# Trainium2: inverse roots of the second and third norm by a power instruction on POOL instead of nine steps on DVE, in a one-core MetaFormer block

## The chip, the cores and the metric

The program runs on one core of one Trainium2 chip. A core has a matrix engine (PE, with its weight loads shown apart as PEld), a vector engine (DVE), a scalar engine (ACT), a general engine (POOL, also called GpSimd) and a queue engine that issues transfers (SP). The engines run side by side and wait for one another by semaphores. The metric is the time of one execution on the device, in microseconds (us).

## The reference, cut to what matters

The input x is 8 images of 64 channels and 32x32 pixels. All in float32:

```python
x = x + conv_attention(ln_over_channels(x, eps=1e-6))      # first norm
t = to_tokens(x)                                            # [8, 1024, 64]
u = layer_norm(t, eps=1e-5)                                 # second norm
rw = softmax(mean(u, axis=1) @ Wr + br)                     # routing of each image over 8 experts
rw = softmax(rw * min(1, capacity / load))
top_w, top_i = top_k(rw, 2); top_w = softmax(top_w)
y = sum_k top_w[k] * (gelu(u @ W1[e_k] + b1[e_k]) @ W2[e_k] + b2[e_k])
out = t + layer_norm(y + u, eps=1e-5) * gamma + beta        # third norm
```

A layer norm subtracts the mean over the 64 channels and multiplies with 1 / sqrt(variance + eps). Attention is over channels: the scores of a head are 8x8.

## The kernel before, in words

The eight images are handled as four pairs p (NP = 4, two images side by side on the 128 partitions, 1024 pixels along the free axis). A norm is over channels, so over partitions. Its sums come out of PE (moment_rows, L888, then transposes, moment_columns, L895) as moments with tokens on the partitions, 16 numbers for each partition and pair (G2 = 16). DVE makes a variance of them, and then an inverse root.

- rsqrt (L511) is nine dependent instructions on DVE, L515 to L525: a shift and a subtraction on the bits for a first guess, a cubic step, and a Newton step. Each waits for the one before through a semaphore (link, L503), which can run other work in that gap (the argument between).
- split3 (L207) cuts the root into three bf16 parts, four instructions L210 to L213. PE transposes them (turn, L912, matmul L913), DVE copies them to RR (rows2, L618, rows3, L779), and PE spreads them over the channels (spread, L924, matmul L927).
- The second norm is done in two groups g of two pairs, 32 columns each. read_moments (L600) writes scaled moments, rstd2 (L609) squares the mean (L611), takes the variance (L612) and calls rsqrt, with residual1 of pair 3 (T, L597) in two gaps for group 0 and rows2(0) in one gap for group 1. POOL's split_group (L422) waits for each root. normal2 (L624, L626) multiplies T with the spread root: UF, with its sum in su. ACT rounds UF to f16 (HI, L308), POOL subtracts (LO, L419), SP copies HI and LO to ST. sw (L697) takes the sums of all pairs and starts the routing (L701 to L747), at whose end POOL gathers the weights of the chosen experts (L437 to L452). PE has 18 filler matmuls (keep_awake, L958, matmul L966) between the sum over tokens (L1027) and the first expert.
- The expert stage is written out by hand in steps (L1109 to L1135): up (L1041, L1053), GELU on ACT (L362), down (L1071, L1080), and among them the third norm of the pair before. ACT squares (L376), PE sums (L891), ACT evacuates (L383), PE transposes (L897), and DVE's rstd3 (L767) makes v (L770) and the root. For pairs 0 to 2 POOL splits it, for pair 3 DVE does (L805). Then rows3, bias2 (L749, L753: the bias of pair p + 2), and scale_z (L785, L788), in the order of DVE's loop from L792. evac_z (L764) takes the expert sums out of PSUM.
- add_residual (L215, L220) adds T to the result, 512 columns at a time, and SP stores each half (L255), waiting in order of pairs and halves. POOL adds all halves of pairs 0 to 2 and half 0 of pair 3; DVE adds the last half.
- Before the last turn PE has nine filler matmuls (keep_awake_at_end, L1086, matmul L1088), before the one of pair 2 seven.

Every engine executes its own list in order. On POOL the list around the change is: split_group(0), split_group(1), LO of pairs 0 and 1, gathers, LO of pairs 2 and 3, and then the loop from L480: gather, split of pair p, additions of pair p - 1.

Of the kernel before, what the change touches and what calls it, by code (L numbers as in the profile page):

```python
# [51 lines left out]
def build_program(nc, x_tok, x_cha, small, w12, consts, constb, out):  # L52
# [11 lines left out]
    with ExitStack() as ctx:  # L64
        def sb(name, shape, dt=F32):
            return ctx.enter_context(nc.sbuf_tensor(name, shape, dt))
# [33 lines left out]
        p1s = sb("p1s", [P, 2, 2, C])  # L100
# [8 lines left out]
        cbs = sb("cbs", [P, NP])  # L109
# [2 lines left out]
        cmp2 = sb("cmp2", [P, 2, 4, 2 * G2])  # L112
        seed = sb("seed", [P, 2 * G2], U32)
        nwt = sb("nwt", [P, 2, 2 * G2])
        r2 = sb("r2", [P, NP, G2])
        v3 = sb("v3", [P, NP, G2])
        r3 = sb("r3", [P, NP, G2])
# [36 lines left out]
        def by_half(ap):  # L154

            return ap.rearrange("p (q h b) -> p h q b", h=2, b=2)
# [16 lines left out]
        def pair_view(ap):  # L173
# [22 lines left out]
        s_sq = [sem(f"s_squared{p}") for p in range(NP)]  # L196
        s_st = [sem(f"s_st{p}") for p in range(NP)]
        s_out = [sem(f"s_out{p}") for p in range(NP)]
        names = ("ones clear onesm wrb sw wcp wcv gram gs tb u p1 p1s s_ps sms exs a_sb b1 b1s mt mts cbs conv t "
                 "row rw mom pow1 pow2 red2 r3 rt rr rb uf hi lo w1p w1h w1l w2p w2v lg rexp1 rexp2 "  # L200
                 "half_tanh rx1 rx2 rx3 wkd top "
                 "g1 g2 c2d mm1 gelu mm2 zs sq3 row3 rw3 mom3 red3 pow3 s3 rt3 rr3 rb3 vv tbeta dve pool").split()
# [4 lines left out]
        def split3(engine, link, b, n, src, done):  # L207

            to = slice(b, b + n)
            link(engine.tensor_copy(R3[:, to, 0, :], src))  # L210
            engine.tensor_tensor(rd[:, to, :], src, R3[:, to, 0, :], ALU.subtract)
            link(engine.tensor_tensor(R3[:, to, 1, :], src, R3[:, to, 0, :], ALU.subtract))
            engine.tensor_tensor(R3[:, to, 2, :], rd[:, to, :], R3[:, to, 1, :], ALU.subtract).then_inc(done, 1)  # L213

        def add_residual(engine, queue, p, h):  # L215

            queue.wait_ge(s["vv"], 2 * p + h + 1)
            queue.wait_ge(s["tbeta"], p + 1)
            cols = slice(h * HALF, (h + 1) * HALF)
            engine.tensor_tensor(OUT[:, p, cols], V[:, p, cols], T[:, p, cols], ALU.add).then_inc(s_fin[2 * p + h], 1)  # L220
# [180 lines left out]
        def _(pool):  # L401
# [18 lines left out]
                                        ALU.subtract).then_inc(s["lo"], 1)  # L420

            def split_group(g):  # L422
                pool.wait_ge(s["pow2"], g + 1)
                if g >= 1:
                    pool.wait_ge(s["rt"], g)
                split3(nc.gpsimd, link, 0, 2, r2[:, 2 * g:2 * g + 2, :], s["r3"])
# [16 lines left out]
            def gather_w2(p, regs):  # L443
# [4 lines left out]
                for k in range(TOP):  # L448
                    for b in range(2):
# [2 lines left out]
                        nc.gpsimd.tensor_tensor(w2g[:, p % 2, b, k, :], w2c[:, bass.ds(e * C, C)],  # L452
                                                wrep.broadcast_to([P, C]), ALU.mult).then_inc(s["g2"], 1)

            nc.gpsimd.memset(ones_m[:, :], 1.0).then_inc(s["onesm"], 1)
            nc.gpsimd.memset(wrbd[:, :], 0.0).then_inc(s["onesm"], 1)
            pool.wait_ge(s["onesm"], 2)
# [22 lines left out]
            for p in range(NP):  # L480
                if p + 2 < NP:
                    gather_w2(p + 2, gather_b1(p + 2))
                if p == NP - 1:
                    break
                pool.wait_ge(s["pow3"], p + 1)
                if p >= 2:
                    pool.wait_ge(s["rt3"], p - 1)
                else:
                    pool.wait_ge(s["rt"], 2)
                split3(nc.gpsimd, link, p % 2, 1, r3[:, p:p + 1, :], s["s3"])  # L490
                if p >= 1:
                    add_residual(nc.gpsimd, pool, p - 1, 0)
                    add_residual(nc.gpsimd, pool, p - 1, 1)
            add_residual(nc.gpsimd, pool, NP - 2, 0)
            add_residual(nc.gpsimd, pool, NP - 2, 1)
            add_residual(nc.gpsimd, pool, NP - 1, 0)


        @block.vector
        def _(dve):  # L500
            count = [0]

            def link(ins, between=None):  # L503

                count[0] += 1
                ins.then_inc(s["dve"], 1)
                if between:
                    between()
                dve.wait_ge(s["dve"], count[0])
# [90 lines left out]
            def read_moments(p):  # L600

                dve.wait_ge(s["mom"], p + 1)
                g, cols = p // 2, slice(p % 2 * G2, (p % 2 + 1) * G2)
                pm = moments_of(moment_bank[p % 2])
                nc.vector.tensor_scalar(by_half(cmp2[:, g, 0, cols]), pm[:, 0], RSQRT ** 0.5 / S_U, None, ALU.mult)
                nc.vector.tensor_scalar(by_half(cmp2[:, g, 1, cols]), pm[:, 1], RSQRT / S_U ** 2,
                                        RSQRT * EPS_T / S_U ** 2, ALU.mult, ALU.add).then_inc(s["red2"], 1)

            def rstd2(g, between=None):  # L609
                dve.wait_ge(s["red2"], 2 * (g + 1))  # L610
                link(nc.vector.tensor_tensor(cmp2[:, g, 2, :], cmp2[:, g, 0, :], cmp2[:, g, 0, :], ALU.mult))  # L611
                link(nc.vector.tensor_tensor(cmp2[:, g, 3, :], cmp2[:, g, 1, :], cmp2[:, g, 2, :], ALU.subtract))  # L612
                if g >= 1:
                    dve.wait_ge(s["pow2"], g)
                rsqrt(cmp2[:, g, 3, :], nwt[:, 0, :], nwt[:, 1, :], seed[:, :],
                      r2[:, 2 * g:2 * g + 2, :].rearrange("p l g -> p (l g)"), s["pow2"], between)

            def rows2(g):  # L618
                dve.wait_ge(s["rt"], g + 1)
                if g >= 1:  # L620
                    dve.wait_ge(s["rb"], 2 * g)
                nc.vector.tensor_copy(RR[:, :, :].rearrange("p l n -> p (l n)"), ps_rt2).then_inc(s["rr"], 1)
# [41 lines left out]
            def residual_between():  # L664

                calls[0] += 1
                if calls[0] in (1, 3):
                    residual1(3, [calls[0] // 2])

            rstd2(0, residual_between)  # L670
            read_moments(2)
            read_moments(3)
            calls[0] = 0

            def rows_between():
                calls[0] += 1
                if calls[0] == 1:
                    rows2(0)

            rstd2(1, rows_between)  # L680
            normal2(0)
            rows2(1)
            normal2(1)
# [83 lines left out]
            def rstd3(p):  # L767
                dve.wait_ge(s["mom3"], p + 1)
                pm = moments_of(pM)
                nc.vector.tensor_scalar(by_half(v3[:, p, :]), pm[:, 0], RSQRT, RSQRT * EPS_T, ALU.mult,  # L770
                                        ALU.add).then_inc(s["red3"], 1)
                dve.wait_ge(s["red3"], p + 1)
                if p == 0:
                    dve.wait_ge(s["pow2"], 2)
                else:
                    dve.wait_ge(s["pow3"], p)
                rsqrt(v3[:, p, :], nwt[:, 0, 0:G2], nwt[:, 1, 0:G2], seed[:, 0:G2], r3[:, p, :], s["pow3"])

            def rows3(p):  # L779
                dve.wait_ge(s["rt3"], p + 1)  # L780
# [27 lines left out]
                    bias2(p + 2)  # L808
            scale_z(NP - 2, 1)
            scale_z(NP - 1, 0)  # L810
            scale_z(NP - 1, 1)
            add_residual(nc.vector, dve, NP - 1, 1)

# [388 lines left out]
```

## Time and profile before

| | us |
|---|---|
| time, median of 3 runs | 119.22 |
| the three runs | 118.45, 119.22, 122.53 |
| span of the profiled execution | 117.0 |
| PE busy | 94.2 |
| DVE busy | 68.5 |
| ACT busy | 50.1 |
| POOL busy | 40.7 |

The span is from the first to the last instruction of one profiled execution. The time of a run also contains what lies around the span; the profiled execution's own time is not listed apart from the three. Busy times are sums over the span, and the engines overlap.

### The profile page before, as it was taken

Reading aid. Unit: us, or ns where it says so; the run is one execution under the profiler, and the core shown is the slowest. Engines: PE = TensorE matmul, PEld = TensorE weight load, DVE = VectorE, ACT = ScalarE, POOL = GpSimd, SP = SyncE. Lnnn points to the kernel's source line nnn. Section 1 sums busy time; section 2 is a strip of 40 time slices with the busy share of each in tenths; the row PEclk is TensorE's granted clock in tenths of the full one; section 3 lists DMA queues with packets and bytes.
Section 4 is the critical chain, followed back from the end, with each engine's and each line's share of the span. In section 5 each row is a group of like instructions: output and inputs, shape, how many; then the busy total and the mean of one; then the engine's idle time right before and its main releaser. Section 6 shows DMA issues by size and latency. Waiting matters only on the chain.

```text
span 117.0 us, 2060 instructions
## 1 busy us (share of the span) xinstructions
PE 94.2 (80%) x626; PEld 46.6 (40%) x629; DVE 68.5 (59%) x276; ACT 50.1 (43%) x76; POOL 40.7 (35%) x93
## 2 busy tenths in 40 slices
PE   0059998989997999676599879999999998989300
PEld 0023497976763546344133223233342333234100
DVE  0299996723374188489869106835185273769850
ACT  0400504615325435407666592892983769050000
POOL 3000724900006000236801649940460550095190
PEclk9999999999999999999558999999999999999985
DMA  3999960000000000002583000560000030004124
GB/s 76 330 421 401 404 248 0 6 0 0 0 0 6 0 0 0 0 0 62 121 203 70 3 3 0 123 146 6 0 3 0 0 150 35 0 17 182 70 90 179
DMA packets 4314, 9.81 MB, mean 84 GB/s; under 512 B 592, under 2 KB 848, under 8 KB 4304
## 3 DMA queue, kind: packets, MB, share of 16 engines
q1 hardware_dynamic: 3728, 8.34, 21.6%
q10 hardware_dynamic: 576, 1.34, 3.2%
q8 instruction: 5, 0.08, 0.3%
q14 instruction: 5, 0.04, 0.1%
HBM read 5.49 MB, written 2.10 MB: 65 GB/s over the span
## 4 chain that ended last, share of the span: by engine, by line
PE 52%; DVE 18%; issue 8%; POOL 6%; DMA 5%; POOLq 5%; ACT 3%; ACTq 0%; DVEq 0%
PE pC L1080 10%; PE pC L886 6%; DMA cst<-consts_dram 5%; POOL XT L220 4%; PE pA L1053 4%; PE pM L956 4%; DVE UF L626 4%; PE pB L1053 4%; PE pS L827 3%; POOLq L437 3%; PE pA L837 3%; PE pM L891 2%; PE pB L949 2%; PE pC L973 2%; PE pS L891 2%
## 5 line engine op out<-in xcount | busy, mean ns | idle before, releaser
L1080 PE MATMUL pC<-H,w2g 128*64 128x512 f32 x64 | 15.8, 603 | 0.5 <-POOL w2g L452 0.5
L362 ACT ACTIVATE H<-pA,b1g 128x1024 f32<-128x1024 f32 x8 | 8.9, 1111 | 8.8 <-PE pA L1053 8.8
L535 DVE BATCH_NORM_STATS2 bst<-XT 128x6 f32<-128x64 f32 x64 | 9.4, 214 | 5.1 <-DMA XT<-x_tok_dram 5.1
L227 POOL TENSOR_TENSOR UT<-XT,rt 128x1024 f32<-128x1024 f32 x3 | 6.7, 2243 | 14.8 <-issue 10.9
L210 POOL CAST R<-r 128x16 bf16<-128x16 f32 (+1 forms) x5 | 1.0, 203 | 29.2 <-DVE r L525 29.2
L220 POOL TENSOR_TENSOR XT<-XT,T 128x512 f32<-128x512 f32 x7 | 9.2, 1334 | 4.0 <-DVE XT L788 4.0
L956 PE MATMUL pM<-cst 128*128 128x480 f32 x6 | 4.6, 904 | 7.2 <-DMA cst<-consts_dram 7.2
L753 DVE TENSOR_TENSOR c<-b2g 64x1 f32<-64x1 f32 x8 | 5.7, 716 | 5.9 <-POOL w2g L452 5.8
L966 PE MATMUL pB<-cstb 128*128 128x512 bf16 x27 | 8.8, 489 | 0.2 <-issue 0.2
L362 ACT ACTIVATE H<-pB,b1g 128x1024 f32<-128x1024 f32 x8 | 8.9, 1117 | 0.0
L419 POOL TENSOR_TENSOR LO<-UF,HI 128x1024 f16<-128x1024 f32 x4 | 8.4, 2128 | 1.2 <-ACT HI L308 1.2
L1053 PE MATMUL pA<-ST,w1hl 128*128 128x512 f16 x32 | 8.3, 382 | 0.5 <-ACT H L362 0.5
L597 DVE SCALAR_TENSOR_TENSOR T<-pC,cbs,X 128x512 f32<-128x512 f32 x8 | 6.0, 751 | 4.5 <-PE pC L886 4.4
L1053 PE MATMUL pB<-ST,w1hl 128*128 128x512 f16 x32 | 8.2, 379 | 0.0
L376 ACT ACTIVATE SQ<-pC,c 128x512 f32<-128x512 f32 x8 | 5.5, 687 | 5.7 <-PE pC L1080 3.9
L886 PE MATMUL pC<-U,MTs 128*128 128x512 f32 x16 | 7.7, 605 | 0.0
L1080 PEld LDWEIGHTS pC<-H,w2g 128*64 128x64 f32 x64 | 4.1, 136 | 6.7 <-issue 5.1
L764 DVE TENSOR_SCALAR U<-pC,c,wsm 128x512 f32<-128x512 f32 x8 | 6.1, 806 | 0.9 <-PE pC L1080 0.9
L788 DVE TENSOR_TENSOR XT<-U,pS 128x512 f32<-128x512 f32 x6 | 4.1, 683 | 4.3 <-PE pS L927 4.2
L308 ACT CAST HI<-UF 128x1024 f16<-128x1024 f32 x4 | 4.2, 1046 | 5.2 <-DVE UF L626 5.0
L439 POOL COPY b1g<-wsm 128x1 f32 x16 | 2.7, 184 | 10.4 <-issue 10.4
L467 POOL TENSOR_TENSOR SQ<-T 128x1024 f32<-128x1024 f32 x1 | 1.9, 1893 | 11.9 <-DVE T L597 11.9
(193 smaller groups left out, 177.1 us busy)
## 6 DMA issues: line engine op xcount, KB each, us to landing
X<-x_cha_dram SPq DMA_DIRECT2D x4, 512.0 KB, 11.3
out_dram<-XT SPq DMA_DIRECT2D x8, 256.0 KB, 2.0
XT<-x_tok_dram SPq DMA_DIRECT2D x3, 512.0 KB, 7.8
ST<-HI SPq DMA_DIRECT2D x8, 128.0 KB, 2.4
ST<-LO SPq DMA_DIRECT2D x8, 128.0 KB, 2.4
w_sb<-w_dram ACTq DMA_DIRECT2D x1, 512.0 KB, 8.1
cstb<-constb_dram ACTq DMA_DIRECT2D x1, 304.0 KB, 9.7
XT<-x_tok_dram ACTq DMA_DIRECT2D x1, 256.0 KB, 4.5
```

Source lines behind the costliest of these rows:

```text
L220: engine.tensor_tensor(OUT[:, p, cols], V[:, p, cols], T[:, p, cols], ALU.add).then_inc(s_fin[2 * p + h], 1)
L227: engine.tensor_tensor(UT[:, p, :, 1:P + 1].rearrange("p j (b c) -> p j b c", b=2), XT[:, p, :].rearrange("p (j b c) -> p j b c", b=2, c=C ...
L362: nc.scalar.activation(H[:, step % 2, b, :], h_ps[b][:, :], ACT.Gelu, bias=b1g[:, p % 2, b, k:k + 1], scale=1.0 / (S_U * S_W)).then_inc(s[ ...
L419: nc.gpsimd.tensor_tensor(LO[:, p, :], UF[:, p, :], HI[:, p, :], ALU.subtract).then_inc(s["lo"], 1)
L535: return nc.vector.bn_stats(bst[:, p // 2, i % (2 * G2), :], XT[:, p, g * C:(g + 1) * C])
L597: nc.vector.scalar_tensor_tensor(out=T[:, p, cols], in0=cv[:, cols], scalar=cbs[:, p:p + 1], in1=X[:, p, cols], op0=ALU.add, op1=ALU.add). ...
L764: nc.vector.tensor_scalar(ZS[:, p, cols], y_ps[:, cols], c2[:, p:p + 1], w("gamma"), ALU.add, ALU.mult).then_inc(s["zs"], 1)
L886: mm(cv[:, cols], MTs[:, p, :], U[:, p, cols], start=True, stop=True).then_inc(s["conv"], 1)
L956: mm(pM[:, 0:480], cf("ident"), cst[:, 0:480], start=True, stop=True)
L966: mm(bank, cb("identb"), cb("sel")[:, 0:HALF], start=True, stop=True)
L1053: last = mm(h_ps[b][:, cols], w1[:, bass.ds(experts[b] * 2 * F + a * F, F)], ST[:, 2 * p + b, cols], start=(a == 0), stop=(a == 1))
L1080: last = mm(half(y_ps[:, cols], b), w2g[:, p % 2, b, k, :], H[:, step % 2, b, cols], start=False, stop=(k == TOP - 1))
```

## The change

The roots of the second and third norm are taken by POOL: one tensor_tensor with the operation pow, whose second operand is a column of -0.5 (mhalf) broadcast over the row. DVE writes plain moments (the factors RSQRT, which only rsqrt needs, go) and ends at the variance. In group 0 of the second norm residual1 of pair 3 now lies in the gap before the variance (half 0) and behind it (half 1); in group 1 rows2(0) follows the variance. POOL's loop also takes the power of pair 3, and then adds pair 2. Half 0 of pair 3 is added by DVE, ahead of the last scale_z. The first norm keeps its nine steps.

```diff
             def split_group(g):
+                pool.wait_ge(s["mh"], 1)
+                pool.wait_ge(s["var2"], g + 1)
+                nc.gpsimd.tensor_tensor(r2[:, 2 * g:2 * g + 2, :], cmp2[:, g, 3, :].rearrange("p (l g) -> p l g", l=2),
+                                        mhalf[:, 0:1].unsqueeze(2).broadcast_to([P, 2, G2]),
+                                        ALU.pow).then_inc(s["pow2"], 1)
                 pool.wait_ge(s["pow2"], g + 1)
...
+            nc.gpsimd.memset(mhalf[:, :], -0.5).then_inc(s["mh"], 1)
...
             for p in range(NP):
                 if p + 2 < NP:
                     gather_w2(p + 2, gather_b1(p + 2))
-                if p == NP - 1:
-                    break
-                pool.wait_ge(s["pow3"], p + 1)
-                if p >= 2:
-                    pool.wait_ge(s["rt3"], p - 1)
-                else:
-                    pool.wait_ge(s["rt"], 2)
-                split3(nc.gpsimd, link, p % 2, 1, r3[:, p:p + 1, :], s["s3"])
+                pool.wait_ge(s["red3"], p + 1)
+                nc.gpsimd.tensor_tensor(r3[:, p, :], v3[:, p, :], mhalf[:, 0:1].broadcast_to([P, G2]),
+                                        ALU.pow).then_inc(s["pow3"], 1)
+                if p < NP - 1:
+                    pool.wait_ge(s["pow3"], p + 1)
+                    if p >= 2:
+                        pool.wait_ge(s["rt3"], p - 1)
+                    else:
+                        pool.wait_ge(s["rt"], 2)
+                    split3(nc.gpsimd, link, p % 2, 1, r3[:, p:p + 1, :], s["s3"])
                 if p >= 1:
                     add_residual(nc.gpsimd, pool, p - 1, 0)
                     add_residual(nc.gpsimd, pool, p - 1, 1)
-            add_residual(nc.gpsimd, pool, NP - 2, 0)
-            add_residual(nc.gpsimd, pool, NP - 2, 1)
-            add_residual(nc.gpsimd, pool, NP - 1, 0)
...
             def rstd2(g, between=None):
                 dve.wait_ge(s["red2"], 2 * (g + 1))
-                link(nc.vector.tensor_tensor(cmp2[:, g, 2, :], cmp2[:, g, 0, :], cmp2[:, g, 0, :], ALU.mult))
-                link(nc.vector.tensor_tensor(cmp2[:, g, 3, :], cmp2[:, g, 1, :], cmp2[:, g, 2, :], ALU.subtract))
-                if g >= 1:
-                    dve.wait_ge(s["pow2"], g)
-                rsqrt(cmp2[:, g, 3, :], nwt[:, 0, :], nwt[:, 1, :], seed[:, :],
-                      r2[:, 2 * g:2 * g + 2, :].rearrange("p l g -> p (l g)"), s["pow2"], between)
+                link(nc.vector.tensor_tensor(cmp2[:, g, 2, :], cmp2[:, g, 0, :], cmp2[:, g, 0, :], ALU.mult), between)
+                nc.vector.tensor_tensor(cmp2[:, g, 3, :], cmp2[:, g, 1, :], cmp2[:, g, 2, :],
+                                        ALU.subtract).then_inc(s["var2"], 1)
+                if between:
+                    between()
...
             def residual_between():
 
                 calls[0] += 1
-                if calls[0] in (1, 3):
-                    residual1(3, [calls[0] // 2])
+                residual1(3, [calls[0] - 1])
...
-            rstd2(1, rows_between)
+            rstd2(1)
+            rows2(0)
             normal2(0)
...
             def rstd3(p):
                 dve.wait_ge(s["mom3"], p + 1)
                 pm = moments_of(pM)
-                nc.vector.tensor_scalar(by_half(v3[:, p, :]), pm[:, 0], RSQRT, RSQRT * EPS_T, ALU.mult,
+                nc.vector.tensor_scalar(by_half(v3[:, p, :]), pm[:, 0], EPS_T, None,
                                         ALU.add).then_inc(s["red3"], 1)
-                dve.wait_ge(s["red3"], p + 1)
-                if p == 0:
-                    dve.wait_ge(s["pow2"], 2)
-                else:
-                    dve.wait_ge(s["pow3"], p)
-                rsqrt(v3[:, p, :], nwt[:, 0, 0:G2], nwt[:, 1, 0:G2], seed[:, 0:G2], r3[:, p, :], s["pow3"])
...
             scale_z(NP - 1, 0)
+            add_residual(nc.vector, dve, NP - 1, 0)
             scale_z(NP - 1, 1)
             add_residual(nc.vector, dve, NP - 1, 1)
```

## Rows read from the trace of the kernel before

**Rows 1.** The page, chain that ended last: shares by engine.
```profile
PE 52%; DVE 18%; issue 8%; POOL 6%; DMA 5%; POOLq 5%; ACT 3%; ACTq 0%; DVEq 0%
```

**Rows 2.** Windows, expert stage: stretch, us; busy us (count) by engine; clock, DMA share, GB/s.
```profile
74.00:97.00 23.00, 22.31 (x126) 7.64 (x124) 12.35 (x36) 15.88 (x21) 9.74 (x35) 1.00 0.21 58
```

**Rows 3.** Timeline, second norm, 48 to 58: start, duration, engine, instruction, [idle before].
```profile
48.46 0.29 PE L913 MATMUL pB<-cstb,R 128*48 128x128 bf16 x2
...
49.09 0.19 DVE L612 TENSOR_TENSOR cmp<-cmp 128x32 f32<-128x32 f32 x1
...
49.74 0.62 PE L927 MATMUL pC<-RR,cstb 48*128 48x128 bf16 x8 [0.99 <-DVE RR L622]
...
51.16 0.19 DVE L525 SCALAR_TENSOR_TENSOR r<-nwt 128x32 f32<-128x32 f32 x1
51.27 1.21 DVE L626 SCALAR_TENSOR_TENSOR UF<-T,pC 128x1024 f32<-128x1024 f32 x1
...
53.07 1.20 DVE L626 SCALAR_TENSOR_TENSOR UF<-T,pA 128x1024 f32<-128x1024 f32 x1
...
53.72 4.22 POOL L419 TENSOR_TENSOR LO<-UF,HI 128x1024 f16<-128x1024 f32 x2 [1.24 <-ACT HI L308]
...
56.60 1.41 DVE L697 TENSOR_TENSOR sw<-wrbd,su 128x64 f32<-128x64 f32 x1
```

**Rows 4.** Groups by line and form, POOL: busy us, mean ns, idle before.
```profile
L220 POOL TENSOR_TENSOR XT<-XT,T 128x512 f32<-128x512 f32 x7 | 9.2, 1334 | 4.0 <-DVE XT L788 4.0
...
L227 POOL TENSOR_TENSOR UT<-XT,rt 128x1024 f32<-128x1024 f32 x3 | 6.7, 2243 | 14.8 <-issue 10.9 <-DVE rt L525 3.9
...
L211 POOL TENSOR_TENSOR rd<-r,R 128x32 f32<-128x32 f32 x2 | 0.5, 244 | 0.2
```

**Rows 5.** Timeline, second norm, group 0, 42 to 47.
```profile
42.38 1.88 PE L886 MATMUL pC<-U,MTs 128*128 128x512 f32 x4
...
43.66 0.75 DVE L597 SCALAR_TENSOR_TENSOR T<-pC,cbs,X 128x512 f32<-128x512 f32 x1
...
46.43 0.19 DVE L525 SCALAR_TENSOR_TENSOR r<-nwt 128x32 f32<-128x32 f32 x1
```

**Rows 6.** Timeline, 18 filler matmuls; window over them: PE, PEld, DVE, ACT, POOL, clock.
```profile
58.55 5.88 PE L966 MATMUL pB<-cstb 128*128 128x512 bf16 x18
...
58.55:64.43 5.88, 5.88 (x21) 2.22 (x23) 4.79 (x40) 3.85 (x5) 0.37 (x2) 0.69 0.58 135
```

**Rows 7.** Timeline, third norm around pair 1, 84 to 97.
```profile
84.66 0.33 DVE L753 TENSOR_TENSOR c<-b2g 64x1 f32<-64x1 f32 x2
...
92.66 2.49 POOL L220 TENSOR_TENSOR XT<-XT,T 128x512 f32<-128x512 f32 x2
...
93.89 0.22 PE L913 MATMUL pS<-cstb,R 128*48 128x128 bf16 x1
...
94.29 1.05 DVE L753 TENSOR_TENSOR c<-b2g 64x1 f32<-64x1 f32 x2
...
96.96 0.64 PE L891 MATMUL pM<-SQ,cst 128*32 128x256 f32 x8 [0.69 <-ACT SQ L376]
```

**Rows 8.** Timeline, tail, 105 to 115.
```profile
105.92 1.26 POOL L220 TENSOR_TENSOR XT<-XT,T 128x512 f32<-128x512 f32 x1 [0.40 <-DVE XT L788]
105.96 1.25 DVE L515 TENSOR_SCALAR seed<-v 128x16 uint32<-128x16 uint32 x1
...
106.30 2.12 PE L1088 MATMUL pA<-cstb 128*128 128x512 bf16 x9
...
108.92 0.17 DVE L210 CAST R<-r 128x16 bf16<-128x16 f32 x1
...
110.82 2.96 POOL L220 TENSOR_TENSOR XT<-XT,T 128x512 f32<-128x512 f32 x2 [3.64 <-DVE XT L788]
...
111.97 0.69 DVE L220 TENSOR_TENSOR XT<-XT,T 128x512 f32<-128x512 f32 x1
112.11 2.50 SPq L255 DMA_DIRECT2D out_dram<-XT  x3
```

More of the change, by code:

```diff
@@ L114, in build_program @@
         nwt = sb("nwt", [P, 2, 2 * G2])
+        mhalf = sb("mhalf", [P, 1])
         r2 = sb("r2", [P, NP, G2])
@@ L198, in build_program @@
         s_out = [sem(f"s_out{p}") for p in range(NP)]
-        names = ("ones clear onesm wrb sw wcp wcv gram gs tb u p1 p1s s_ps sms exs a_sb b1 b1s mt mts cbs conv t "
+        names = ("ones mh var2 var3 clear onesm wrb sw wcp wcv gram gs tb u p1 p1s s_ps sms exs a_sb b1 b1s mt mts cbs conv t "
                  "row rw mom pow1 pow2 red2 r3 rt rr rb uf hi lo w1p w1h w1l w2p w2v lg rexp1 rexp2 "
@@ L604, in read_moments @@
                 pm = moments_of(moment_bank[p % 2])
-                nc.vector.tensor_scalar(by_half(cmp2[:, g, 0, cols]), pm[:, 0], RSQRT ** 0.5 / S_U, None, ALU.mult)
-                nc.vector.tensor_scalar(by_half(cmp2[:, g, 1, cols]), pm[:, 1], RSQRT / S_U ** 2,
-                                        RSQRT * EPS_T / S_U ** 2, ALU.mult, ALU.add).then_inc(s["red2"], 1)
+                nc.vector.tensor_scalar(by_half(cmp2[:, g, 0, cols]), pm[:, 0], 1.0 / S_U, None, ALU.mult)
+                nc.vector.tensor_scalar(by_half(cmp2[:, g, 1, cols]), pm[:, 1], 1.0 / S_U ** 2,
+                                        EPS_T / S_U ** 2, ALU.mult, ALU.add).then_inc(s["red2"], 1)
             def rstd2(g, between=None):
                 dve.wait_ge(s["red2"], 2 * (g + 1))
-                link(nc.vector.tensor_tensor(cmp2[:, g, 2, :], cmp2[:, g, 0, :], cmp2[:, g, 0, :], ALU.mult))
-                link(nc.vector.tensor_tensor(cmp2[:, g, 3, :], cmp2[:, g, 1, :], cmp2[:, g, 2, :], ALU.subtract))
-                if g >= 1:
-                    dve.wait_ge(s["pow2"], g)
-                rsqrt(cmp2[:, g, 3, :], nwt[:, 0, :], nwt[:, 1, :], seed[:, :],
-                      r2[:, 2 * g:2 * g + 2, :].rearrange("p l g -> p (l g)"), s["pow2"], between)
+                link(nc.vector.tensor_tensor(cmp2[:, g, 2, :], cmp2[:, g, 0, :], cmp2[:, g, 0, :], ALU.mult), between)
[3 more added lines that the diff above has]
+                    between()
             def rows2(g):
@@ L672, in _ @@
             read_moments(3)
[L673 to L678, printed above, removed]
-            rstd2(1, rows_between)
+            rstd2(1)
+            rows2(0)
             normal2(0)
```

## The prediction

> **What bounds the kernel now.** I read the chain that ended last, then the stages in windows, then each place that the diff touches in the timeline. The shares of the chain give PE 52%, DVE 18% and POOL 6% [rows 1]: PE is the bound on average, and the question is where it waits for the code that changes. In the expert stage PE is busy 22.31 of 23 us at the full clock [rows 2]; there a shorter inverse root is worth only what PE idles. That leaves four places.
>
> (a) Second norm, group 1. DVE ends the variance at 49.28 and the root r at 51.35 (51.16 + 0.19). PE has had the spread factors of pair 0 ready since 49.74 + 0.62 = 50.36, but the product UF of pair 0 starts only at 51.27, behind the nine steps. UF of pair 1 starts at 53.07, which is 1.72 after r: POOL's split, PE's turn and DVE's copy lie between. The sum sw starts at 56.60 and takes 1.41 for 64 columns, ending at 58.01, just after POOL's two subtractions LO (53.72 + 4.22 = 57.94) [rows 3]. So LO ends this stage, not the last UF. (b) Second norm, group 0, which has cover. (c) Third norm of pair 1, where POOL's additions hold DVE up. (d) The tail, from v at 105.75.
>
> **What a power costs.** The trace has no power instruction; its price is the unknown. Below: a plain two-input POOL operation of the same 32 columns takes 0.244 us [rows 4], one of 16 columns hardly less. Beneath that nothing can lie, since an instruction must at least read and write its columns. A power is a routine of many steps for each column, so I take the price as if each of its columns cost 32 plain ones: for 32 columns the row of 1024, 2.24 us [rows 4], for 16 columns an addition of 512, 1.27 (the row's mean of 1.334 holds one that was stretched; two others took 2.49 together). The ordinary price of 32 columns is nearest in size but not in work; I go by the work of nine dependent steps, 9 x 0.244 = 2.2, which is the same. Above, I keep twice the value, 4.5 and 2.5. This is a choice between ends far apart and carries the whole forecast.
>
> The Trainium skill (GPSIMD Engine Reference, section 7, Performance pitfalls) says that a dependent fp32 chain pays 4 cycles per element and step on POOL. No run here shows it; by it nine steps would be 36 cycles at 1.2 GHz, 30 ns a column, an estimate of 1.2 us for 32 columns and 0.7 for 16, and a routine of twenty steps 2.4 and 1.3. The same page (section 3) calls POOL the wrong engine for ordinary elementwise work, which speaks against this change. The sum below does not use it.
>
> **Group 0: hidden.** The new order puts T of pair 3, half 0, between the square and the variance. PE ends the four passes of that pair's product at 42.38 + 1.88 = 44.26, its first half about 43.4; T takes 0.75, so the variance comes at about 44.35, after T. Then the power, with a handover of 0.07 before it, to 46.66; r came at 46.62 [rows 5]. POOL's four split steps take 4 x 0.244 and their waits, 1.1, to 47.75, and PE turns the result at 48.46 [rows 3], after other work in its own order. Cover is 0.7 us: above a price of 2.24 + 0.7 = 2.95 this goes on the path. T half 1 starts 0.3 earlier, hidden behind PE's row sums. I count 0.
>
> **Group 1.** UF of pair 0 starts at about 50.3 instead of 51.27: 0.97 earlier, and so may HI and LO of pair 0 be. The split starts after the power: 49.28 + 0.07 + 2.24 = 51.59 against 51.35, so UF of pair 1 starts at 53.31 (in general 51.07 + price). From the start of pair 0's UF to the start of its LO it is 53.72 - 51.27 = 2.45, with HI on ACT between; a LO takes 2.11. So pair 1's LO ends at 51.07 + price + 2.45 + 2.11, at 57.87 against 57.94: the gain at sw is 2.3 less the price, at most 0.97, and with 2.24 it is 0.07. What PE hands on of it depends on its clock. The 18 filler matmuls before the first expert take 5.88 us, because the granted clock starts at its lower level (0.5, 1.2 GHz): it is 0.69 on average over these 5.88 us, so low for 0.62 of them, until about 62.2 [rows 6]. If it rises at the same instant in the new kernel, those started earlier run slow, and about half of a gain here is lost. I count 0.05 (for a plain price 0.5 to 0.97, and 0.75 in the sums below).
>
> **Third norm, pairs 0 and 2: hidden.** The nine steps go from DVE (for pair 1 they ended 1.87 after v), and POOL is idle there. Pair 1's split ends where its additions start, about 92.7, and PE turns it at 93.89, in its own order [rows 7]: slack 1.2, so the turn costs nothing up to 1.87 + 1.2 = 3.1 us. Pair 0 has the same pattern, and pair 2 is followed by filler matmuls.
>
> **Pair 1, POOL's additions.** Behind the split POOL adds two halves, 2.49 us from 92.66, to 95.15. DVE's addition of two 64x1 columns (L753), beside it, takes 1.05 from 94.29, where pair 2's takes 0.33: it is held 0.72, until POOL's add ends. Behind it wait the evacuation of pair 2, its square on ACT, and PE, idle 0.69 before 96.96 [rows 7]. With the power in place of the nine steps the additions end at 93.29 + price, at 94.56 instead of 95.15. DVE is then held for 0.27 instead of 0.72, and PE's idle time shrinks by about 0.46. A price of 1.0 or less frees all 0.69 (I count 0.65); above 1.87 it becomes a loss, one for one.
>
> **Tail.** v is done at 105.92. The nine steps take until 108.89, 1.08 of it because the first, L515, lasts 1.25 beside POOL's add of 105.92 (1.26). DVE's split starts at 108.92 [rows 8]. After the change POOL is free at 105.9 (its additions of pair 1 come 0.6 earlier), so the power ends at 105.99 + 1.27 = 107.26. But the next instruction in POOL's queue is the very add that held L515; nothing holds it back, so it starts at once and DVE's split, two SBUF inputs, waits 1.26 for it. The split starts at 107.29 + price = 108.55: gain 1.63 less the price, 0.36. The stall does not go, it moves from the seed to the split. The gain is capped at 1.2 by the nine filler matmuls, which end at 106.30 + 2.12 = 108.42 [rows 8], ahead of the turn behind the split.
>
> The Trainium skill (SBUF — State Buffer, section Who interferes with whom) says that DVE and POOL share a port pair under an exclusive lock and that issue order decides who waits; the 1.25 us of L515 and the 1.41 of sw agree. If DVE came first by that rule, the tail would gain what the next rival gives.
>
> **The last additions.** Before, POOL's two run 110.82 to 113.78, DVE's from 111.97, and the last store is issued from SP at the end of 112.11 + 2.50 = 114.61 [rows 8]. Now DVE's add (3,0) meets POOL's add (2,1), waits until 112.09 and ends 0.69 later, 112.78; the last scaling follows (0.6), then add (3,1), to 114.11. That is 0.33 later than 113.78, but only one store, not two of 0.33 to 0.43, is then left: issued by 114.48 instead of 114.61, gain 0.1.
>
> **Sum.** 0.05 + 0.46 + 0.36 + 0.1 = 1.0 us off a span of 117.0. The profiled execution has no time of its own in the list; its span stands 1.45 below the lowest (118.45) and 2.2 below the median of the three, start and end around it included. Off the median 119.22 that is 118.2.
>
> **Rivals.**
> A cheap power (chance 0.20). POOL's flat price for short operations speaks for it: 32 columns cost hardly more than 16. At half my price (1.2 and 0.7): 0.75 + 0.65 + 0.93 + 0.1 = 2.4, 116.8. At the plain price: 0.75 + 0.65 + 1.2 + 0.1 = 2.7, 116.5. Winning the lock in the tail adds at most 1.26, less the cap, and gives that time at my own price too. Against it: a power is no single arithmetic step.
>
> A dear power, the other side (0.36). Place: POOL's queue in both groups of the second norm. From a price of 2.95 group 0's power holds back group 1's, which stands behind it on the same engine; at 4.5 it runs 44.42 to 48.9, the split to 50.0, the second power to 54.5, 3.15 later than r now, and UF of pair 1 with HI and LO behind it make sw 2.8 late. Pair 1 of the third norm loses 0.77, the tail 1.63 - 2.5 = -0.87, the end gains 0.1: 4.3 us, 123.5. It decides from 1.25 times my price (2.8 and 1.6), where gain turns to loss; at 1.7 times it costs 2.3 (121.5). For it: the nine DVE steps, each 0.2, may be fewer than what the routine does for each column. A first use that loads code would come on top; group 0 hides 0.7 of it.
>
> The clock (0.04). The order of PE's work around 50 to 55 shifts; if the fall at 55.3 stays out, the filler shrinks from 5.88 to 18 x 0.236 = 4.2 us (the 9 of the tail take 2.12 [rows 8]). The routing chain of DVE and ACT beside it keeps part of these 1.7; an estimate of 1.2 comes out: 117.0. Against it: the fall follows the thin stretch of 49 to 54, which stays thin.
>
> **How the numbers follow.** Forecast 0.40, cheap 0.20, dear 0.36, clock 0.04. Within 2% (2.4 us) is what this measurement can tell from no change. Faster by more: the cheap case and half of the clock, 0.22. Slower by more: the dear case from 1.75 times my price, 0.32. The rest 0.46. The forecast's own range is 117.2 to 119.6 (price 0.7 to 1.3 times mine). The full range must reach into both, 116.2 to 123.2.
>
> **What the profile after would show.** Powers on POOL of 128x32 at 2.2 and of 128x16 at 1.3 us; UF of pair 0 right behind the spread of PE, near 50.3; the long L753 of pair 1 at 0.4; DVE's first split step in the tail at 1.3 to 1.4 us beside POOL's add, and the last add on DVE some 0.3 us after where POOL's stood. Powers over 2.8 us, or a DVE that waits for POOL at the rows of group 0, would prove the forecast wrong upward; powers under 1.2, or a split in the tail that is not held, downward.

## The result, and the profile after

The changed kernel is slower: ratio 1.058 to the kernel before, 95% interval 1.049 to 1.066. Its median is 127.3 us (4 runs), against 120.7 for the kernel before beside it. Some executions of either kernel are some 3 us longer than the others, and the ratio is taken from the shorter ones (125.1 and 126.6 us of the changed kernel). The forecast was 118.2 with a range up to 123.2.

The page of the changed kernel, first the engines (busy us, share, instructions), then who leads the chain that ended last:

```profile
span 127.7 us, 2013 instructions
PE 100.8 (79%) x629; PEld 49.8 (39%) x629; DVE 60.8 (48%) x223; ACT 50.2 (39%) x76; POOL 61.3 (48%) x99
...
PE 36%; POOL 23%; DVE 13%; issue 13%; DMA 5%; POOLq 4%; ACT 3%; ACTq 0%; DVEq 0%
POOL r L426 8%; POOL r L491 7%; PE pC L879 5%; DMA cst<-consts_dram 5%; PE pC L1073 4%; PE pM L949 4%; POOL XT L221 4%; PE pS L820 3%; POOLq L443 3%; PE pC L966 3%; PE pA L830 2%; PE pA L1046 2%; DVE UF L631 2%; ACT H L363 2%; DVE XT L780 1%
```

POOL had 6% of the chain [rows 1] and now has 23%, most of it in two lines: L426 and L491, the powers. DVE is 8 us less busy than the 68.5 of before, and it buys nothing. The price that the forecast had to guess, in the groups by form (busy us, mean ns, idle before):

```profile
L491 POOL TENSOR_TENSOR r<-v,mhalf 128x16 f32<-128x16 f32 x4 | 11.6, 2899 | 9.0 <-DVE v L768 9.0
L426 POOL TENSOR_TENSOR r<-cmp,mhalf 128x32 f32<-128x32 f32 x2 | 10.8, 5425 | 7.3 <-DVE cmp L618 7.3
```

2.90 us for 16 columns and 5.43 for 32, where the forecast took 1.27 and 2.24 and kept 2.5 and 4.5 as its upper end. A plain operation of 32 columns takes 0.244 [rows 4]. The nine DVE steps that a power replaces took 2.03 us for 32 columns (49.32 to 51.35 in the kernel before) and 1.87 for 16, from v of pair 1.

The second norm, from the timeline (start, duration, engine, instruction, [idle before]), to be held against [rows 3] and [rows 5]:

```profile
48.16 0.18 DVE L618 TENSOR_TENSOR cmp<-cmp 128x32 f32<-128x32 f32 x1
48.49 5.43 POOL L426 TENSOR_TENSOR r<-cmp,mhalf 128x32 f32<-128x32 f32 x1 [7.27 <-DVE cmp L618]
53.02 0.19 DVE L618 TENSOR_TENSOR cmp<-cmp 128x32 f32<-128x32 f32 x1
55.00 5.42 POOL L426 TENSOR_TENSOR r<-cmp,mhalf 128x32 f32<-128x32 f32 x1
55.10 0.29 PE L906 MATMUL pB<-cstb,R 128*48 128x128 bf16 x2 [2.63 <-POOL R L214]
61.59 0.41 PE L906 MATMUL pB<-cstb,R 128*48 128x128 bf16 x2 [2.68 <-POOL R L214]
62.24 1.20 DVE L631 SCALAR_TENSOR_TENSOR UF<-T,pA 128x1024 f32<-128x1024 f32 x1
65.91 0.98 DVE L695 TENSOR_TENSOR sw<-wrbd,su 128x64 f32<-128x64 f32 x1
```

The reader is to see three things. PE's first turn waits 2.63 us for POOL, where it had 0.7 us of slack. The second variance is ready at 53.21, but its power starts at 55.00, behind the first power and split in POOL's queue. And UF of pair 1 starts only at 62.24; LO of pair 1, the UF of the pairs behind and then sw wait for it.

Pair 1 of the third norm, to be held against [rows 7]:

```profile
98.51 2.89 POOL L491 TENSOR_TENSOR r<-v,mhalf 128x16 f32<-128x16 f32 x1 [1.64 <-DVE v L768]
102.39 2.49 POOL L221 TENSOR_TENSOR XT<-XT,T 128x512 f32<-128x512 f32 x2
102.93 1.97 DVE L751 TENSOR_TENSOR c<-b2g 64x1 f32<-64x1 f32 x2
106.52 0.64 PE L884 MATMUL pM<-SQ,cst 128*32 128x256 f32 x8 [1.61 <-ACT SQ L377]
```

DVE's addition of two 64x1 columns now takes 1.97 us instead of 1.05, until POOL's additions end, and PE idles 1.61 instead of 0.69. The tail, against [rows 8]:

```profile
113.68 2.50 POOL L221 TENSOR_TENSOR XT<-XT,T 128x512 f32<-128x512 f32 x2
115.55 0.17 DVE L768 TENSOR_SCALAR v<-pM 128x16 f32<-128x16 f32 x1
116.13 2.90 POOL L491 TENSOR_TENSOR r<-v,mhalf 128x16 f32<-128x16 f32 x1
119.00 1.26 POOL L221 TENSOR_TENSOR XT<-XT,T 128x512 f32<-128x512 f32 x1
119.07 1.23 DVE L211 CAST R<-r 128x16 bf16<-128x16 f32 x1 [3.35 <-POOL r L491]
120.85 0.24 PE L906 MATMUL pB<-cstb,R 128*48 128x128 bf16 x1 [2.64 <-DVE R L214]
```

The power waits 0.4 us for POOL's additions of pair 1, takes 2.90, and then the cast is held by POOL's next addition, as forecast.

**Where the time went.** The profiled execution of the changed kernel ran its first matmuls at half speed, which put everything behind them 4 us later than in that of before; it is not the change's doing. So I count from a mark that both have ahead of the first changed instruction that matters: DVE's read of the moments of pair 1 (L605 before, L611 after), at 42.81 before and 46.76 after. The table gives us from that mark, from the timelines. "Squares" is PE's sum of squares of the third norm (L891), "turn" PE's last one (L913).

| kernel | sw done | squares, pair 0 | squares, pair 2 | v of pair 3 | last turn | end |
|---|---|---|---|---|---|---|
| before | 15.20 | 34.49 | 54.15 | 62.94 | 66.84 | 74.19 |
| changed | 20.13 | 39.19 | 59.76 | 68.79 | 74.09 | 80.94 |
| e1, cheap operation | 14.10 | 32.74 | 51.74 | 60.54 | 63.12 | 69.97 |
| e2, second norm only | 20.12 | 39.01 | 58.68 | 67.48 | 71.37 | 78.73 |
| e3, third norm only | 15.20 | 33.82 | 54.47 | 63.56 | 68.87 | 76.19 |
| e4, additions only | 15.19 | 33.82 | 53.50 | 62.29 | 66.19 | 73.03 |

Between before and changed: the second norm costs 4.9 us at sw and 4.7 behind it; pair 1 adds 0.9; from the squares of pair 2 to v of pair 3 another 0.24 is lost, as PE's turn of pair 2 now waits for POOL's split (0.17 us of idle time at 113.78); from v to the last turn 1.4; and the last additions give 0.5 back. Together 6.75, and the ratio, 0.058 of some 119, is 6.9.

The clock is the other thing that changed in this stretch: the granted clock is at its lower level for some 14 us here (57 to 71), against 7 before (55.3 to 62.2). It adds little: the second power already ends 5.1 us later from the mark (60.42 is 13.66 behind it, r came 8.54 behind it), and from the end of sw to the squares of pair 0 it is 19.06 us against 19.29 before.

### The profile page after: what moved, and what is told of

Its sections match the earlier page's. It is cut to its first block, busy times and chain, and to the rows that moved or that the text cites. A ratio compares the mean times of both kernels' runs of the same rounds, so it can differ in the third digit from the quotient of the medians.

```text
span 127.7 us, 2013 instructions
## 1 busy us (share of the span) xinstructions
PE 100.8 (79%) x629; PEld 49.8 (39%) x629; DVE 60.8 (48%) x223; ACT 50.2 (39%) x76; POOL 61.3 (48%) x99
## 4 chain that ended last, share of the span: by engine, by line
PE 36%; POOL 23%; DVE 13%; issue 13%; DMA 5%; POOLq 4%; ACT 3%; ACTq 0%; DVEq 0%
POOL r L426 8%; POOL r L491 7%; PE pC L879 5%; DMA cst<-consts_dram 5%; PE pC L1073 4%; PE pM L949 4%; POOL XT L221 4%; PE pS L820 3%; POOLq L443 3%; PE pC L966 3%; PE pA L830 2%; PE pA L1046 2%; DVE UF L631 2%; ACT H L363 2%; DVE XT L780 1%
## 5 line engine op out<-in xcount | busy, mean ns | idle before, releaser
L491 POOL TENSOR_TENSOR r<-v,mhalf 128x16 f32<-128x16 f32 x4 | 11.6, 2899 | 9.0 <-DVE v L768 9.0
L426 POOL TENSOR_TENSOR r<-cmp,mhalf 128x32 f32<-128x32 f32 x2 | 10.8, 5425 | 7.3 <-DVE cmp L618 7.3
L949 PE MATMUL pM<-cst 128*128 128x480 f32 x6 | 5.5, 1061 | 7.2 <-DMA cst<-consts_dram 7.2
L959 PE MATMUL pB<-cstb 128*128 128x512 bf16 x28 | 10.1, 530 | 0.0
L751 DVE TENSOR_TENSOR c<-b2g 64x1 f32<-64x1 f32 x8 | 6.6, 830 | 5.8 <-POOL w2g L458 5.8
L221 POOL TENSOR_TENSOR XT<-XT,T 128x512 f32<-128x512 f32 x6 | 7.5, 1266 | 1.8 <-DVE XT L780 1.8
L309 ACT CAST HI<-UF 128x1024 f16<-128x1024 f32 x4 | 4.2, 1046 | 10.5 <-DVE UF L631 10.5
L906 PE MATMUL pB<-cstb,R 128*48 128x128 bf16 x5 | 0.9, 261 | 8.0 <-POOL R L214 5.3
```

Source lines behind the costliest of these rows:

```text
L426: nc.gpsimd.tensor_tensor(r2[:, 2 * g:2 * g + 2, :], cmp2[:, g, 3, :].rearrange("p (l g) -> p l g", l=2), mhalf[:, 0:1].unsqueeze(2).broad ...
L491: nc.gpsimd.tensor_tensor(r3[:, p, :], v3[:, p, :], mhalf[:, 0:1].broadcast_to([P, G2]), ALU.pow).then_inc(s["pow3"], 1)
L949: mm(pM[:, 0:480], cf("ident"), cst[:, 0:480], start=True, stop=True)
L959: mm(bank, cb("identb"), cb("sel")[:, 0:HALF], start=True, stop=True)
```

## The experiments

**e1: the same placement with a cheap operation.** It leaves out the inverse roots: the power becomes a multiplication.

```diff
-                                        ALU.pow).then_inc(s["pow2"], 1)
+                                        ALU.mult).then_inc(s["pow2"], 1)
...
-                                        ALU.pow).then_inc(s["pow3"], 1)
+                                        ALU.mult).then_inc(s["pow3"], 1)
```

> The changed kernel with a multiplication in place of each power, so the roots are wrong and everything else stands where the change put it (it leaves out the inverse roots of the second and third norm). Theory P (the price of the power alone makes the loss): faster than the kernel before by 2 to 3 us, ratio 0.975 to 0.985, with roots of 0.24 us (32 columns) and 0.22 us (16). Theory Q (POOL is the wrong place: handovers, its queue and the shared port cost by themselves): no faster than before, ratio 1.00 or more.

Measured: ratio 0.964 (0.954 to 0.974), with the multiplications at 0.24 and 0.22 us. Everything that the change moves is a gain once the instruction is cheap, so the theory that POOL's place itself costs falls. The gain is larger than the 2 to 3 us expected. By the table it is 1.1 at sw, 0.66 more up to the squares of pair 0, 0.66 at pair 1, 1.3 in the tail and 0.5 at the end. The rows behind the second of these:

```profile
55.27 1.16 DVE L695 TENSOR_TENSOR sw<-wrbd,su 128x64 f32<-128x64 f32 x1
56.49 0.43 PE L1020 MATMUL pS<-sw,ones_m 128*128 128x64 f32 x2 [1.60 <-DVE sw L695]
56.76 4.05 PE L959 MATMUL pB<-cstb 128*128 128x512 bf16 x18
62.10 1.03 PE L1046 MATMUL pA<-ST,w1hl 128*128 128x512 f16 x4 [0.74 <-issue]
```

The 18 matmuls take 4.05 us instead of 5.88 [rows 6]: the granted clock stayed at 1.00 throughout 50 to 62 here. e4, below, shows 0.67 us for this alone.

**e2: the power for the second norm only.** The third norm's root, POOL's loop and the last additions are those of before.

```diff
-                pool.wait_ge(s["red3"], p + 1)
-                nc.gpsimd.tensor_tensor(r3[:, p, :], v3[:, p, :], mhalf[:, 0:1].broadcast_to([P, G2]),
-                                        ALU.pow).then_inc(s["pow3"], 1)
...
+                rsqrt(v3[:, p, :], nwt[:, 0, 0:G2], nwt[:, 1, 0:G2], seed[:, 0:G2], r3[:, p, :], s["pow3"])
...
-            add_residual(nc.vector, dve, NP - 1, 0)
```

> Power on POOL for the second norm only; third norm and last additions as before. Theory P: two powers of 5.4 us in a row on POOL make the sum over tokens 4.9 us later than before, and 4.7 us of it arrive at the end: ratio 1.035 to 1.045. Theory Q, with a loss shared evenly between the six powers: some 2.3 us, ratio 1.02.

Measured: ratio 1.036 (1.026 to 1.047). In the table sw is 4.92 later, and 4.5 of it arrives at every later mark. Two of the six powers carry two thirds of the loss.

**e3: the power for the third norm only.**

```diff
-                rsqrt(v3[:, p, :], nwt[:, 0, 0:G2], nwt[:, 1, 0:G2], seed[:, 0:G2], r3[:, p, :], s["pow3"])
...
+                pool.wait_ge(s["red3"], p + 1)
+                nc.gpsimd.tensor_tensor(r3[:, p, :], v3[:, p, :], mhalf[:, 0:1].broadcast_to([P, G2]),
+                                        ALU.pow).then_inc(s["pow3"], 1)
```

> Power on POOL for the third norm only; second norm and last additions as before. Theory P: 0.9 us at pair 1 (POOL's additions hold DVE longer), 0.2 at pair 2, 1.4 in the tail: 2.5 us, ratio 1.015 to 1.025. If the power were hidden wherever POOL is idle, only the tail would show: 1.4 us, ratio 1.012.

Measured: ratio 1.023 (1.012 to 1.033), 2.7 us. Against e4, whose profile has the same early filler (33.82 at the squares of pair 0 in both), the squares of pair 2 are 0.97 later, v of pair 3 1.27 and the last turn 2.68. So pair 1 costs 1.0, pair 2 0.3 and the tail 1.4, and "hidden wherever POOL is idle" falls.

**e4: both last additions on DVE, nothing else.**

```diff
-            add_residual(nc.gpsimd, pool, NP - 1, 0)
...
             scale_z(NP - 1, 0)
+            add_residual(nc.vector, dve, NP - 1, 0)
             scale_z(NP - 1, 1)
```

> The kernel before with both additions of the last pair on DVE and nothing else changed. From the traces of both kernels, the stretch from the last turn on PE to the end is 7.35 us before and 6.85 after: 0.5 us faster, ratio 0.996. By the prediction's own working 0.1 us faster, ratio 0.999. If DVE's wait for POOL's port weighs more: slower by 0.3 us or more.

Measured: ratio 0.996 (0.989 to 1.004), which can't be told from no change by times. The profile shows 6.84 us from the last turn to the end, against 7.35. The timeline of its end:

```profile
114.02 1.26 POOL L220 TENSOR_TENSOR XT<-XT,T 128x512 f32<-128x512 f32 x1 [3.63 <-DVE XT L787]
...
114.58 1.26 DVE L220 TENSOR_TENSOR XT<-XT,T 128x512 f32<-128x512 f32 x1
115.76 0.68 DVE L787 TENSOR_TENSOR XT<-U,pA 128x512 f32<-128x512 f32 x1
116.47 0.69 DVE L220 TENSOR_TENSOR XT<-XT,T 128x512 f32<-128x512 f32 x1
```

DVE's first addition is held as forecast (1.26 where the free one takes 0.69), yet the end comes earlier: the last addition ends 0.17 us later from the turn (4.30 against 4.13), but from there to the end it is 2.54 us instead of 3.22, with one store left to issue and not two.

This profile shows one thing more. Up to the tail its order of work is that of the kernel before, and sw is done at the same 15.19 us from the mark, but the granted clock stayed at 1.00 in every microsecond from 47 to 70:

```profile
62.19 4.05 PE L966 MATMUL pB<-cstb 128*128 128x512 bf16 x18
```

The squares of pair 0 are 0.67 us earlier than before (33.82 against 34.49), and so they are in e3 and e9. The 1.83 us that the 18 matmuls save is worth 0.67 there.

**e5: the price by itself.** Four powers on POOL near the start, where it idles.

```diff
+            for at, n in ((0, 1), (1, 8), (9, 16), (25, 32)):
+                nc.gpsimd.tensor_tensor(probe[:, at:at + n], ones_m[:, 0:n], mhalf[:, 0:1].broadcast_to([P, n]), ALU.pow)
```

> The kernel before with four extra powers on POOL near its start, where POOL idles, over 1, 8, 16 and 32 columns of ones; nothing reads their results. From the changed kernel's 2.90 us for 16 columns and 5.42 for 32: 0.16 us for each column and 0.37 fixed, so 0.5, 1.6, 2.9 and 5.4 us. If the first power pays for loading code, the one over 1 column takes a microsecond or more. If the routine is shorter on easy values, ones cost less than the real variances did.

```profile
L463 POOL TENSOR_TENSOR probe<-ones_m,mhalf 128x32 f32<-128x32 f32 x1 | 5.4, 5415 | 0.0
L463 POOL TENSOR_TENSOR probe<-ones_m,mhalf 128x16 f32<-128x16 f32 x1 | 2.9, 2896 | 0.0
L463 POOL TENSOR_TENSOR probe<-ones_m,mhalf 128x8 f32<-128x8 f32 x1 | 1.7, 1653 | 0.0
L463 POOL TENSOR_TENSOR probe<-ones_m,mhalf 128x1 f32<-128x1 f32 x1 | 0.6, 559 | 0.1
```

A straight line: (5415 - 1653) / 24 = 157 ns for each column and 0.40 us fixed. The first power of the program costs no more than the line says (0.559 by 0.40 + 0.157), so there is no first use to pay, and powers of ones cost what those of real variances cost (2.896 and 5.415 us, against 2.899 and 5.425). The one run took 118.4 us, where the kernel before took 118.1 to 119.1, so 10.5 us of powers in POOL's idle time cost nothing that shows.

**e6: the changed kernel without the hold in the tail.**

```diff
                 if p >= 1:
+                    if p == NP - 1:
+                        pool.wait_ge(s["s3"], NP)
                     add_residual(nc.gpsimd, pool, p - 1, 0)
```

(the wait stands ahead of the two additions of pair 2)

> The changed kernel, but POOL's first addition of pair 2 waits until DVE has split pair 3. If POOL's addition holds DVE's first split step (1.23 us against 0.17 to 0.2), that step falls to 0.2 and the end comes 1.1 us earlier: ratio to the kernel before 1.048 instead of 1.058. If DVE's step is long for another reason, it stays at 1.2 and the time is that of the changed kernel or later.

The times are no verdict: the four runs lie between 123.8 and 129.0 us, and no ratio came out of them. The profile decides: the cast takes its usual time, and from the start of v to the turn on PE it is 4.25 us instead of 5.30, and the end is 0.84 earlier from the mark (80.10 against 80.94).

```profile
116.06 0.17 DVE L770 TENSOR_SCALAR v<-pM 128x16 f32<-128x16 f32 x1
119.58 0.17 DVE L211 CAST R<-r 128x16 bf16<-128x16 f32 x1 [3.35 <-POOL r L491]
```

**e7: the same wait in the kernel before.**

```diff
+            pool.wait_ge(s["s3"], NP)
             add_residual(nc.gpsimd, pool, NP - 2, 0)
```

> The kernel before, with the same wait: POOL's first addition of pair 2 starts behind DVE's split of pair 3. The seed step L515 of pair 3 falls from 1.25 to 0.17 us, and the turn on PE comes 1.1 us earlier, just behind the nine filler matmuls: ratio 0.991. If the filler or the later additions take it back: 1.000.

Measured: ratio 0.995 (0.990 to 1.000). The seed falls from 1.25 us [rows 8] to 0.17, the turn comes 1.07 earlier after v, and the end 0.97 earlier in the profile. The times give 0.6 us where 1.1 were expected; the expected ratio of 0.991 is still inside the interval.

```profile
105.97 0.17 DVE L516 TENSOR_SCALAR seed<-v 128x16 uint32<-128x16 uint32 x1
...
106.31 2.12 PE L1089 MATMUL pA<-cstb 128*128 128x512 bf16 x9
108.59 0.24 PE L914 MATMUL pB<-cstb,R 128*48 128x128 bf16 x1 [0.17 <-DVE R L213]
```

**e8: more filler on PE in the second norm of the kernel before.**

```diff
-            keep_awake(5)
+            keep_awake(7)
             turn2(1)
...
-            keep_awake(5)
+            keep_awake(9)
             pe.wait_ge(s["sw"], 1)
```

> The kernel before with filler matmuls of the second norm raised from 5 and 5 to 7 and 9, in stretches where PE idles. In the run with the cheap operation the granted clock did not fall around 55 to 62, and the 18 filler matmuls took 4.05 instead of 5.88 us. If PE's idle time decides that, the clock stays at its upper level here too, the 18 take 4.1 us, and 1.2 us come out at the end: ratio 0.99. If not, the clock falls as before and the ratio is 1.000 or, through the longer filler, slightly above.

Measured: ratio 1.002 (0.994 to 1.010). The windows (us, busy of PE, PEld, DVE, ACT, POOL, then the clock) and the filler behind them:

```profile
55.00:56.00 1.00, 1.00 (x10) 0.54 (x7) 1.00 (x3) 0.90 (x2) 1.00 (x1) 0.95 0.88 205
56.00:57.00 1.00, 1.00 (x4) 0.30 (x2) 0.97 (x3) 0.91 (x2) 1.00 (x2) 0.50 0.29 66
...
59.00:60.00 1.00, 1.00 (x6) 0.41 (x4) 0.67 (x3) 0.18 (x2) 0.00 (x0) 0.85 0.91 213
```

```profile
58.80 4.30 PE L966 MATMUL pB<-cstb 128*128 128x512 bf16 x18
```

The clock still falls to its lower level, but rises some 3 us earlier, and the 18 matmuls take 4.30 us. Of these 1.6 us only 0.4 is left at the squares of pair 0 (the first expert matmul is 0.97 earlier from the mark, the squares 0.41). What caps the gain stands some 12 us behind the start of the filler in the kernel before, with POOL's LO of pairs 2 and 3:

```profile
71.03 4.21 POOL L419 TENSOR_TENSOR LO<-UF,HI 128x1024 f16<-128x1024 f32 x2
71.18 4.08 DVE L753 TENSOR_TENSOR c<-b2g 64x1 f32<-64x1 f32 x2 [3.74 <-POOL w2g L452]
```

Two small additions of the bias (0.32 us alone) last 4.08 here, until POOL is done, and DVE evacuates pair 0 (U, L764) only behind them. They end 32.45 us from the mark before and 32.46 in e8, since they hang on the routing and on POOL and not on the filler. U starts 0.40 behind them before, when it waits for PE, and 0.03 behind them in e8. So a faster PE alone can gain 0.4 in this stretch and no more. In e4 the additions end 0.25 earlier as well, at 32.20, since PE's sum over tokens ahead of the routing took 0.43 us at the full clock instead of 0.69; that makes its 0.67.

**e9: POOL's additions of pair 0 moved behind the bias of pair 3, in the kernel before.**

```diff
                 if p >= 1:
+                    if p == 1:
+                        pool.wait_ge(s["c2d"], NP)
                     add_residual(nc.gpsimd, pool, p - 1, 0)
```

> The kernel before, with POOL's two additions of pair 0 waiting until DVE has added the bias of pair 3. If they are what holds L753 (1.05 us where 0.33 is usual) and PE behind it (idle 0.69), L753 falls to 0.33 and 0.65 us come out at the end: ratio 0.9945. If the stretch behind takes it back, the ratio is 1.000.

Measured: ratio 0.991 (0.986 to 0.995). From squares 0 to squares 2 it is 18.93 us in the profile, against 19.66 before: 0.73 gained, where 0.65 was expected (the times give 1.1). DVE's addition is back to its usual time, and POOL's run behind it:

```profile
97.77 0.31 DVE L755 TENSOR_TENSOR c<-b2g 64x1 f32<-64x1 f32 x2
...
98.16 2.51 POOL L220 TENSOR_TENSOR XT<-XT,T 128x512 f32<-128x512 f32 x2 [1.97 <-DVE c L755]
```

**e10: LO of pair 1 moved behind sw, in the kernel before.**

```diff
             low(0)
+            pool.wait_ge(s["sw"], 1)
             low(1)
```

> The kernel before, with POOL's subtraction LO of pair 1 waiting until DVE has made sw. sw falls from 1.41 to 0.2 us, since nothing holds it. But LO then runs beside the routing chain, whose first subtraction with two SBUF inputs (L705) is held in its place, until about 2.1 us after sw: of 1.2 us only 0.3 come out, ratio 0.997. If the hold does not recur, 0.990.

Measured: ratio 0.989 (0.982 to 0.996), more than expected.

```profile
56.39 0.22 DVE L698 TENSOR_TENSOR sw<-wrbd,su 128x64 f32<-128x64 f32 x1
...
57.15 4.64 PE L967 MATMUL pB<-cstb 128*128 128x512 bf16 x18
...
57.91 0.99 DVE L706 TENSOR_TENSOR rout<-rout,rsm 128x64 f32<-128x64 f32 x1
```

sw takes 0.22 instead of 1.41 [rows 3], and the hold recurs at the next operation with two SBUF inputs, as expected. But the filler behind sw takes 4.64 us instead of 5.88, and 0.8 us are left at the end of the profile, where 0.3 were expected. The routing chain is 0.44 earlier from the mark at its last such subtraction (18.10 against 18.54), which is the 1.21 of sw less the 0.77 of the new hold. The other 0.4 is what e8 has too: U of pair 0 starts 0.04 behind the held additions of the bias (32.06 against 32.02 from the mark) and not 0.40.

**e11 and e12: the moves together, with the nine steps kept on DVE.** e11 joins e7, e9 and the additions of e4; e12 adds e10.

> The kernel before (nine steps on DVE everywhere) with three moves: POOL's additions of pair 0 behind the bias of pair 3, POOL's first addition of pair 2 behind DVE's split of pair 3, both additions of pair 3 on DVE. Separate gains in the traces: 0.65, 1.06 and 0.5 us: 2.2 us together, ratio 0.981.

> The same three moves, and LO of pair 1 behind sw. With 0.3 us from that: 2.5 us, ratio 0.979; if the later LO delays the transfers or the routing chain, no better than without it, 0.981 to 0.985.

Measured: e11 0.975 (0.968 to 0.983), e12 0.970 (0.966 to 0.974), with a median of 115.8 us. e12 beats both kernels, by the order of the work alone. In its profile the end is 71.07 us from the mark, against 74.19 before: 0.8 at the squares of pair 0, 0.7 more at pair 1, 1.1 in the tail, 0.5 at the end. Together 3.1 us, where the ratio gives 3.6 and 2.5 were expected; LO's move alone gave 0.8 and not 0.3. The profile of e11 ends 72.05 us from the mark, 2.1 earlier than before, as expected.

## Why the prediction was wrong

**The step that failed** is the price of a power: "as if each of its columns cost 32 plain ones", 2.24 and 1.27 us. Measured are 5.43 and 2.90, a column at 157 ns. A plain column is 2.2 ns by the row of 1024 [rows 4], so a power costs 71 plain columns, not 32. The support given for it, nine dependent steps of 0.244, mixed up instructions with steps inside one: those 0.244 are mostly fixed cost (32 columns at 2.2 ns are 0.07), nothing showed that each step inside one instruction pays it again, and nothing said that there are nine. Worse, the upper end was set at twice the guess. No row bounded the price from above. The dear rival, with a chance of 0.36, ended at 4.5 and 2.5 and gave 123.5 even so, above the range's 123.2; what came was dearer than both.

By the Trainium skill (GPSIMD Engine Reference, section 7, Performance pitfalls), 4 cycles for each dependent fp32 step, 157 ns at 1.2 GHz would be about 47 steps in a row; that is an estimate, and no run shows the routine's inside. The same page's section 3.1 keeps elementwise work on DVE. It spoke against this change, and here the trace agrees: 5.43 us for the power against 2.03 for the nine DVE steps.

**The workings held at the measured price.** Put into the forecast's own formulas, 5.43 and 2.90 give:
- Group 0 and 1. The first power would end at 44.42 + 5.43 = 49.85 and its split at 50.9, the second power at 56.4, 5.0 later than r came, which by the same working is 4.7 at sw. Measured: the second power ends at 60.42, which is 13.66 from the mark, against 8.54 before: 5.1 later. This is the mechanism of the dear rival, the queue of POOL, at a higher price than it was given.
- LO ends the stage, not UF. This held: sw again ran until POOL's subtraction ended, 0.98 us long.
- Pairs 0 and 2 hidden. Pair 0 was: from its squares to those of pair 1, with the power of pair 0 between them, it is 9.30 us against 9.31 before. Pair 2 was not, by 0.24; the forecast gave it no limit of its own.
- Pair 1, one for one above 1.87: 1.03. Measured 0.91, and 0.97 by e3.
- Tail, 1.63 less the price: a loss of 1.27. Measured 1.40. The forecast had POOL free when v came; at this price it was not (0.34 us more of waiting), while the hold swallowed the cast's own 0.2. The hold itself moved from the seed to the split as said: 1.23 us, and e6 takes it away. The reason given, two SBUF inputs, does not fit: the step that was held is the cast, with one.
- The last additions: forecast 0.1, measured 0.5. The hold of DVE was right (1.26). The addition ended 4.30 us after the turn, where the forecast's 0.33 on top of 4.13 gives 4.46, so the last store was issued 0.30 earlier (4.66 after the turn against 4.96) and not 0.13. The other 0.2 lies between that issue and the end, where the forecast expected nothing; why it is shorter no run shows.
- Together: 4.7 + 1.03 + 1.27 - 0.1 = 6.9, against 6.75 in the profiles. That is closer than its terms are, since pair 2, left out, and the end, undervalued, err in opposite directions.

**The other rivals.** The cheap rival's plain price was wrong by a factor of 22 at 32 columns, but its consequences were run in e1: it was forecast at 2.7 us and gave 4.2 in the profile. Of the missing 1.5, 0.66 is the granted clock that did not fall, and 0.4 the last additions; the rest is spread. The clock was a rival of its own, given 0.04 and priced at 1.2 us; in the changed kernel it fell. What its absence is worth the runs show: 0.67 us, in e4, e3 and e9, whose order of work is that of before up to this place. So a shorter second norm is not needed for it, and what decides whether the clock falls stays open.

## What to carry to other kernels

An operation that the trace has never shown has no upper end in the trace, however many rows lie near it: run it once by itself, in idle time of its engine, over two widths, before moving anything onto it (e5 takes a few lines). Count an instruction moved to another engine by what stands behind it in that queue: two powers in a row cost more than four that stood alone. And where a small operation on DVE lasts until a long one on POOL ends, a semaphore that lets the small one go first can take the wait away; three such waits and one addition moved gave 3% here (e12).

## What was not expected of the hardware

- The price of a power on POOL: 0.40 us and 157 ns for each column, for ones and for real variances alike, also for the first one (e5).
- The first matmuls of an execution may run at half speed although the granted clock reads 1.00. Four passes of 512 columns took 3.78 us in the changed kernel's profile (and in e4's), and 2.50 in e2's:

```profile
10.69 3.78 PE L966 MATMUL pC<-w_sb,cst 64*128 64x512 f32 x4
```

```profile
10.79 2.50 PE L972 MATMUL pC<-w_sb,cst 64*128 64x512 f32 x4
```

- The wait for POOL's port strikes operations as small as a cast of 16 columns or an addition of one, and costs what is left of POOL's instruction: 1.23 us for the cast, and 0.75 and 1.21 for the two additions that make up the 1.97, each beside one of POOL's. The longest is in both kernels: two additions beside LO of pairs 2 and 3, 4.08 us where 0.32 is usual; no run here moves it. The Trainium skill (SBUF — State Buffer, section Who interferes with whom) calls it an exclusive lock that goes by issue order; e6, e7, e9 and e10, which change only the order, agree.
- The granted clock can differ between executions with the same order of work. In the stretch of 55 to 62 it fell to its lower level before, and in e8 and e10, and stayed at 1.00 in e3, e4 and e9, whose order up to there is that of before but whose first matmuls ran slow (the mark comes at 46.7 to 46.9 us, against 42.8). It also stayed at 1.00 in e1. What decides it stays open.
